# A channel product that waits for its squares in two halves, and a low part placed in front of a combination

## What is computed

```python
x  = L0_attn_x
xn = _layernorm(x)
s  = _L0_attn_ref(xn, ...)          # RWKV block: time mix, then channel mix
g  = _silu(_L0_ffn_ref(xn, ...))    # 8 experts, each token goes to one
return x + s * g
```

```python
kf  = jnp.einsum('btc,hc->bth', xk2, Wfk)
kf  = jnp.square(jax.nn.relu(kf))
kv  = jnp.einsum('bth,ch->btc', kf, Wfv)
rkv = jax.nn.sigmoid(jnp.einsum('btc,oc->bto', xr2, Wfr)) * kv
```

## Time and profile before

| | us |
|---|---|
| median of 3 runs (lowest, highest) | 1070.64 (1070.15, 1071.73) |
| the profiled execution's own time | 1072.04 |
| its span from first to last instruction | 1070.3 |
| PE busy, share of the span | 1016.8, 95% |
| DVE busy, share | 875.6, 82% |
| ACT busy, share | 688.2, 64% |
| POOL busy, share | 392.4, 37% |

### The profile page before, as it was taken

One profiled execution on the slowest core, in us unless ns is written; L12 is line 12 of the kernel. 1 busy time (PEld: TensorE's weight loads), 2 busy tenths in 40 slices (PEclk: granted clock), 3 DMA queues, 4 the chain that ended last, 5 costly groups with the idle time before them and its releaser, 6 DMA issues.

```text
span 1070.3 us, 18410 instructions
## 1 busy us (share of the span) xinstructions
PE 1016.8 (95%) x5410; PEld 835.7 (78%) x5410; DVE 875.6 (82%) x1750; ACT 688.2 (64%) x1232; POOL 392.4 (37%) x421
## 2 busy tenths in 40 slices
PE   4899999999999999999999899999997999999996
PEld 4668787676877777787786768677786999999985
DVE  5899899998989899898999979787554777777765
ACT  2558566586856768576684847667364666666653
POOL 3204057100001011000200368766515666666653
PEclk9889999999999999999999999999998999999999
DMA  7543320101201011010101102018613333333310
GB/s 257 175 139 119 97 81 21 40 20 41 59 0 59 0 59 58 1 59 0 59 30 30 39 22 60 1 52 250 211 29 93 102 113 113 113 114 110 108 47 22
DMA packets 59474, 80.29 MB, mean 75 GB/s; under 512 B 7678, under 2 KB 46719, under 8 KB 59394
## 3 DMA queue, kind: packets, MB, share of 16 engines
q1 hardware_dynamic: 48130, 54.16, 16.0%
q0 software_dynamic: 11280, 25.32, 8.0%
HBM read 64.38 MB, written 26.36 MB: 85 GB/s over the span
## 4 chain that ended last, share of the span: by engine, by line
PE 67%; ACT 12%; DVE 11%; issue 4%; POOL 3%; another core or an unknown queue 1%; DMA 1%; SPq 0%; ACTq 0%; DVEq 0%; POOLq 0%
PE psKV L1002 18%; PE psM L939 13%; PE psM L1076 11%; PE psM L953 5%; ACT arena L663 3%; ACT arena L560 3%; PE psM L978 2%; PE psM L971 2%; PE psM L973 2%; ACT arena L659 2%; PE psKV L1096 1%; PE psKV L1098 1%; PE psKV L1097 1%; PE psT L904 1%
## 5 line engine op out<-in xcount | busy, mean ns | idle before, releaser
L1002 PE MATMUL psKV<-arena 128*128 128x256 f32 x1024 | 233.3, 383 | 8.9 <-ACT arena L663 8.9
L1002 PEld LDWEIGHTS psKV<-arena 128*128 128x128 f32 x1024 | 193.8, 191 | 50.0 <-issue 22.7
L439 POOL TENSOR_SCALAR lnw<-mv 128x4 f32<-128x4 f32 x32 | 19.4, 608 | 468.7 <-DVE mv L1396 468.7
L1076 PE MATMUL psM<-arena 128*128 128x128 f32 x1136 | 142.4, 279 | 4.7 <-DVE arena L1647 3.4
L1076 PEld LDWEIGHTS psM<-arena 128*128 128x128 f32 x1136 | 134.9, 194 | 6.9 <-DVE arena L1647 4.4
L607 ACT ACTIVATE arena<-psM 128x512 f32<-128x512 f32 x64 | 36.5, 588 | 133.5 <-PE psM L939 133.5
L522 POOL DMA_INDIRECT out_dram<-arena,list_sb x71 | 87.6, 1234 | 74.3 <-issue 41.8
L1413 DVE SCALAR_TENSOR_TENSOR arena<-arena,vecs 128x512 f32<-128x512 f32 x160 | 110.0, 746 | 0.1
L971 PE MATMUL psM<-mix_hi,wfk_hi 128*128 128x512 f32 x256 | 105.5, 412 | 0.2
L973 PE MATMUL psM<-mix_hi,wfk_lo 128*128 128x512 f32 x256 | 100.6, 393 | 0.0
L560 ACT ACTIVATE arena<-s_ring,cf 128x256 f32 (+1 forms) x128 | 66.4, 595 | 47.8 <-POOL cf L444 47.8
(11 more groups left out here) (210 smaller groups left out, 2372.5 us busy)
## 6 DMA issues: line engine op xcount, KB each, us to landing
arena<-in_x SPq DMA_DIRECT2D x16, 512.0 KB
desk<-in_xT SPq DMA_DIRECT2D x16, 512.0 KB, 4.0
xs_rows<-s_ring SPq DMA_DIRECT2D x16, 512.0 KB
xs_rows<-in_x SPq DMA_DIRECT2D x16, 512.0 KB
desk<-in_x SPq DMA_DIRECT2D x15, 512.0 KB, 5.3
desk<-in_W SPq DMA_DIRECT2D x8, 512.0 KB
arena<-in_W SPq DMA_DIRECT2D x8, 512.0 KB, 7.4
out_dram<-arena,list_sb POOLq DMA_INDIRECT x71
```

Of the source, the lines that this page charges most:

```text
L1002: ins = pe.matmul(psKV[:, j // 2, (j % 2) * C:(j % 2 + 1) * C], kf2[:, h, j * P:(j + 1) * P], wfv[:, h, :], start=(h == 0), stop=(h == HC ...
L1076: ins = pe.matmul(psM[:, t % 2, f * P:(f + 1) * P], w1_t[t % 2][:, k, f * P:(f + 1) * P], xnT[t % 2][:, k, :], start=(k == 0), stop=(k == ...
```

## The change

The first edit splits one wait in two: `channel_out(b, 0)` starts when four squares of the sequence are done, and waits for all eight in front of its fifth chunk. The second moves one DVE instruction: for tile 68 (`TILES - 3`), the low part of tile 70 is made in front of `combine(68)` and not behind it.

```diff
             def channel_out(b, j):
                 if j == 0:
-                    pe.wait_ge(S["sq_done"], b * HC + HC)
+                    pe.wait_ge(S["sq_done"], b * HC + HC // 2)
 
                     if not (isinstance(b, int) and b == 0):
                         wait_run(pe, S["s_mult"], b)
                 for h in range(HC):
+                    if j == 0 and h == HC // 2:
+                        pe.wait_ge(S["sq_done"], b * HC + HC)
                     ins = pe.matmul(psKV[:, j // 2, (j % 2) * C:(j % 2 + 1) * C], kf2[:, h, j * P:(j + 1) * P],
                                     wfv[:, h, :], start=(h == 0), stop=(h == HC - 1))
...
+                if t == TILES - 3:
+                    split_h(t + 2, (i + 2) % RING)
                 combine(t, i, g)
-                if t < TILES - 2:
+                if t < TILES - 3:
                     split_h(t + 2, (i + 2) % RING)
```

## The result

The changed kernel takes 1059.10 us (median of 4 runs, 1058.96 to 1060.14) against 1071.09 (4 runs, 1070.15 to 1071.73) before: a ratio of 0.9891, 95% interval 0.9874 to 0.9908. That is 12.0 us less; the forecast was 10.05 less and 1060.6.

A forecast was written before the change was run, and what follows sets the result against it. PE was taken to bound the loop rounds, lacking 0.64 us each to a wait for squares. First edit 8.4 plus second 1.65 gave 10.05 us, so a median of 1060.6; range for 8 in 10: 1057.5 to 1064.5.

The forecast's parts named there:

- Half is lost to a wait that takes the old one's place: Rival, chance 0.20: another PE-DVE meeting point is as tight, a loop round wins only 0.35 us; 1063.1 us in all.
- All of PE's time passes on: Rival, chance 0.10: DVE catches up in every round, rounds 3 to 14 win 0.88 us each; 1057.1 us in all.
- Rounds 1 and 2: First edit in the first two rounds: PE's earlier product passes on whole, 0.68 and 0.67 us.
- rounds 11 and 12: First edit: round 11's add has no idle time, so 0; round 12's idles 0.34, so 0.35 us.
- The loop round, 0.70: First edit, rounds 4 to 10: each wins what the residual add (L1550) wins, 0.70 us; ends 0.55 and 0.88.
- Nothing is left over there: Loop round: the projection's chunk 1 weight load follows the residual add (L1550) closely, so there is no further slack.
- its cap of 0.66 to 0.74: Loop round: the residual add (L1550) can move earlier by 0.66 to 0.74 us and no further, DVE's preceding work being the limit.
- Rounds 13 and 14, 0.88 each: First edit: no routing sums here and the add idles 2.61 us, so PE's whole 0.88 us each, 1.76 together.
- The tail, 1.65: Second edit, last tiles: the moved low part ends PE's wait before tile 70's last product; 1.65 us, bounds 1.2 and 1.7.
- a shorter first matmul: Tail: tile 70's first matmul, no longer having waited, takes 0.28 us and not 0.38, adding 0.10 us.
- Everything between 800 and 1054 us should only move: The experts' steady part, untouched by the edits, was claimed to shift in time without changing length.
- Stops called remote: Rivals on ACT's stops at L802, 8.0 us in two: three or more added, slower (0.04); vanish or one added (0.03).

The follow-up runs named there:

- squares_only: The kernel before with the first edit (split wait on squares) and without the second: 1047.33 us against 1056.91 before on the same chip.
- late_dve: The changed kernel plus an extra DVE instruction in front of the residual add of rounds 4 to 10: 1047.61 us against 1056.91 before on the same chip.
- tail_only: The kernel before with the second edit (tile 70's low part moved) and without the first: 1056.44 us against 1056.91 before on the same chip.

## Why the prediction was right

**Place and sign.** Every place came out as written: the wait on squares gone, no wait in the product's middle, no idle time at the loop's adds (but for 0.21 in round 4), over 1 us (1.30) at round 3's weight load, a new one of 0.93 in round 11, idle adds in 13 and 14, the last product back to back. "Half is lost to a wait that takes the old one's place" fell with loop rounds of 44.77; "All of PE's time passes on" holds for the loop (0.85 of 0.88) but not for rounds 3 and 11.

**Rounds 1 and 2** were forecast at 0.68 and 0.67 and gave 0.67 each. **Round 3** gave 0 as forecast, and rounds 11 and 12 together 0.48 where 0.35 was forecast.

**The loop round, 0.70, was too small.** The second channel product of round 3 starts 2.18 earlier than before, that of round 10 8.16 earlier (533.72 and 525.56): 5.98 / 7 = 0.85. The step that failed is "Nothing is left over there: L1550 ends at 390.18 + 1.22 = 391.40, and the weight load of that projection's chunk 1 starts at 391.51". Behind L953's start the add moved from 3.85 to 3.95, so it won 0.10 less than PE, as its cap of 0.66 to 0.74 says. But PE took the difference. Chunk 1's weights came 391.51 - 389.93 = 1.58 behind the projection's start before and come 386.04 - 384.35 = 1.69 behind it now, and the matmul that needs them starts 1.80 behind both times. So something was left over: the load stood 0.22 ahead of its matmul and could slip by 0.11 without cost, and 0.74 + 0.11 = 0.85 was to be had. The 0.11 that remain are no slack. In round 7 of squares_only the load stands only 0.07 ahead (385.64 and 385.71), and the next matmul follows after 0.46 and not 0.43. late_dve shows too that all is used up now. This one term is 7 x 0.15 = 1.05 us.

**Rounds 13 and 14, 0.88 each, were too large** for the profiled execution: 0.32 and 0.39 by the starts of turn2, since each add came 0.55 late, behind a semaphore of PE that was late by as much. With adds on time (squares_only, round 14: 44.17 against 45.02) the round gives 0.85. The mechanism was right; the late add is the size that was missing, 1.0 us.

**The tail, 1.65,** gave 1.58 in the trace and 1.5 to 1.7 over all pairs of T. The 0.10 for a shorter first matmul did not come: it takes 0.38 in the changed kernel too.

**The sum.** 10.05 forecast; in the trace the edits' own places have 0.67 + 7.82 + 1.58 = 10.07, where the loop's excess and the late adds cancel. That the forecast's 10.05 is met so closely is luck; both terms were off by a us, in opposite directions. Without late adds it is 0.67 + 9.0 + 1.6 = 11.3. The rest of the 12.0, 0.8 ahead of round 1 and 1.2 in the experts' part, lies where nothing was changed and within what executions of one kernel differ by. "Everything between 800 and 1054 us should only move" holds to that 1.2.

**Stops called remote.** None was added in front of L802: 8.0 us before, 6.6 after, each time two. In front of L810, which the forecast did not count, it is 5.7 before and 6.4 after, again two each.

## What to carry to other kernels

Where an engine waits for the last of several inputs and uses them one by one, put the wait in front of the first use of the late ones; what it costs there is only how late they are. Then look for the next engine that the bound engine waits for and count its idle time, and add the part of the weights' lead over their matmul that can be given up (0.11 of 0.22 us here): that much a late hand-over may slip for free. When an instruction moves, look at what then stands between it and its readers; an early add that left its statistics behind two mixes cost 1.2 us in one round. To learn whether a stretch is level, lengthen it by a known 0.4 us in the kernel before and after: it went through in full in one and vanished in the other.

## What was not expected of the hardware

The same program is 14 us to 16 us faster on one chip: the kernel before has a median of 1056.91 there, 1071.09 to 1072.55 on the others. The rounds are equal (L953 of round 15 at 752.91 in tail_only there, at 752.40 in the first trace of before); the difference lies in the experts' part. Ten us of it, by PE's busy time and the granted clock, first before on the slower chip, then tail_only on the faster (same columns as above):

```profile
815.00:825.00 10.00, 5.43 (x20) 4.33 (x21) 2.54 (x5) 1.34 (x3) 7.15 (x7) 0.62 0.36 103
```

```profile
815.00:825.00 10.00, 10.00 (x91) 10.00 (x90) 7.49 (x16) 6.52 (x15) 7.90 (x7) 1.00 0.34 101
```

On the slower chips PE is busy for half of the time and ACT for 1.34 us of 10 while POOL issues the first gathers, and the stops called remote belong to it; on the faster one the trace has none. A second such stretch, of some 4 us, follows near tile 62. This is more than the whole change is worth, so only comparisons on one chip mean anything here. What the engines lack in these stretches the traces don't say.

The other surprise is the late add. DVE has stood ready for 2.2 us, PE's next matmul starts on time, and the semaphore that tells DVE of the finished product comes 4.17 us behind the product's start instead of 3.63, in five of six cases of one program and in none of its variants.
